# Scores and values of an attention block rebuilt: f32 keys on two row halves, probabilities stationary, row sums from a ones column

## The reference

```python
x = x + nin(attention(group_norm(x)), wo, bo)      # phase 1: softmax(q k / 8) v over all 1024 tokens
t = x.reshape(16, 1024, 64)
u = layernorm(t)
t = t + softmax(causal(u Wq (u Wk)' / 8)) u Wv      # phase 2: the same size, lower triangle only
u = layernorm(t)
logits = u gate_w' + gate_b                         # 32 experts choose 8 tokens each per image
t = t + scatter(top8 weights * ffn(top8 pooled u))
```

## Time and profile before

| | us |
|---|---|
| median of 3 runs | 1145.77 |
| lowest, highest | 1144.09, 1167.03 |
| span of the profiled execution | 1163.8 |
| PE busy | 954.6 (82%), 4402 matmuls |
| PE weight loads | 506.2 (43%) |
| DVE busy | 768.3 (66%) |
| ACT busy | 543.1 (47%) |
| POOL busy | 507.5 (44%) |

### The profile page before, as it was taken

How to read it: one execution, slowest core, us unless ns; L and a number is a source line. 1 busy time by engine, 2 the same in 40 slices (tenths; PEclk the granted TensorE clock), 3 DMA queues, 4 the chain that set the end, 5 groups by cost and what they waited for, 6 DMA issues and landing times. The chain is left out here.

```text
span 1163.8 us, 15672 instructions
## 1 busy us (share of the span) xinstructions
PE 954.6 (82%) x4402; PEld 506.2 (43%) x4402; DVE 768.3 (66%) x1741; ACT 543.1 (47%) x1110; POOL 507.5 (44%) x342
## 2 busy tenths in 40 slices
PE   2676798989798989898889989898989899876466
PEld 1333354545354544454444535454544444443235
DVE  4647677777777777776776777777766776645134
ACT  2233355565556446363545545463635455543320
POOL 0051536464646364554444454554444554642200
PEclk9987799999899879797888879797878878985657
DMA  1000000000000000010100000010100010100098
GB/s 37 0 1 9 1 10 24 10 24 10 23 9 23 9 18 14 0 32 0 32 0 23 9 20 11 0 32 0 32 0 24 9 44 16 42 1 23 24 216 238
DMA packets 58654, 30.34 MB, mean 26 GB/s; under 512 B 34775, under 2 KB 55415, under 8 KB 58623
## 3 DMA queue, kind: packets, MB, share of 16 engines
q1 hardware_dynamic: 58623, 29.95, 10.2%
HBM read 15.26 MB, written 10.49 MB: 22 GB/s over the span
## 5 line engine op out<-in xcount | busy, mean ns | idle before, releaser
L832 ACT ACTIVATE probs<-scores 128x512 f32<-128x512 f32 (+3 forms) x496 | 246.6, 513 | 302.9 <-PE scores L684 293.7
L911 POOL TENSOR_TENSOR prob_sum<-prob_sum,probs 128x1024 f32<-128x1024 f32 (+1 forms) x144 | 296.7, 2061 | 145.8 <-ACT probs L832 138.9
L1069 DVE TENSOR_REDUCE maxima<-maxima_in 128x1 f32<-128x512 f32 (+3 forms) x496 | 266.3, 580 | 78.6 <-PE maxima_in L664 75.4
L682 PE MATMUL scores<-queries_lo,keys_hi 72*128 72x512 f32 (+3 forms) x496 | 228.8, 463 | 21.9 <-DVE queries_lo L1061 21.6
L664 PE MATMUL maxima_in<-keys,queries 128*128 128x512 f32 (+3 forms) x496 | 200.3, 462 | 38.3 <-DVE maxima L1069 36.1
L684 PE MATMUL scores<-queries,keys 128*128 128x512 f32 (+3 forms) x496 | 200.0, 404 | 0.0
L698 PE MATMUL values_out<-probs,x_sb 128*64 128x512 f32 x512 | 165.1, 729 | 0.0
L664 PEld LDWEIGHTS maxima_in<-keys,queries 128*128 128x128 f32 x496 | 108.7, 227 | 125.4 <-DVE maxima L1069 71.9
L682 PEld LDWEIGHTS scores<-queries_lo,keys_hi 72*128 72x128 f32 x496 | 108.3, 218 | 105.2 <-issue 53.1
L887 POOL TENSOR_TENSOR ln<-ln,minus_half 128x8 f32<-128x8 f32 x32 | 52.7, 1648 | 187.9 <-DVE ln L1050 187.9
L684 PEld LDWEIGHTS scores<-queries,keys 128*128 128x128 f32 x496 | 108.9, 219 | 9.1
(11 more groups left out here) (167 smaller groups left out, 1244.4 us busy)
## 6 DMA issues: line engine op xcount, KB each, us to landing
x_sb<-in_x SPq DMA_DIRECT2D x16, 256.0 KB, 3.0
u_all<-u_sb SPq DMA_DIRECT2D x16, 256.0 KB, 2.4
t_scratch<-t SPq DMA_DIRECT2D x16, 256.0 KB, 2.9
total<-t_scratch SPq DMA_DIRECT2D x16, 256.0 KB, 4.6
w_sb<-in_w SPq DMA_DIRECT2D x1, 2080.0 KB
logits_scratch<-rows_mixed SPq DMA_DIRECT2D x16, 128.0 KB, 1.9
lg<-logits_scratch SPq DMA_DIRECT2D x4, 512.0 KB, 3.7
out<-total SPq DMA_DIRECT2D x16, 128.0 KB, 2.0
```

The source lines that it names most:

```text
L682: pe.matmul(bank, keys_hi[s][q][:, key_cols(t)], queries_lo[s][q][:, lo:hi], start=not diagonal, stop=False, skip_group_check=diagonal)
L832: nc.scalar.activation(probs[:, t % NP, lo:hi], scores[:, (u + (s - 1) * len(UNITS_1)) % NST, 0:hi - lo], ACT.Exp, scale=SCALE).then_inc(e ...
L911: nc.gpsimd.tensor_tensor(view(total[:, :]), view(total[:, :]), view(new), ALU.add).then_inc(rows_added, 1)
L1069: V.reduce_max(maxima[s][:, c, h:h + 1], maxima_in[:, p % NM, 0:w * P], AX.X).then_inc(maxima_taken, 1)
```

## The change

The attention is written anew; the expert part stays.

- *Scores and maxima in plain f32.* Keys lie in 64 rows twice: key tiles 0, 2, 4, 6 in the upper 64 partitions and 1, 3, 5, 7 in the lower (`keys`, 512 columns), queries in both halves. A pair of key tiles is two f32 matmuls of 64 rows, one in each half of the array, into two of three PSUM banks (L669). The row maximum comes in by a second, fp32r matmul for each (L672). No high and low parts are left, nor the instructions that made them.
- *Values.* A block of probabilities (128 keys x 128 queries) is stationary, the 64 value columns and a column of ones move (L690, 65 columns). The output has queries on partitions, and the row sums as its 65th column. `prob_sum`, POOL's sums, the copy of `values_out`, f.rs and f.out are gone; the output weights are multiplied into the values ahead (w_v, steps x.v and y.v).
- *Maxima.* Two f32 matmuls for each query tile (L652) into one buffer of two banks. DVE reduces both banks at once, in phase 2 together with an added mask (L975, L978). The maxima are turned and spread over 128 rows by PE (L628).
- *Order.* Slots are halves of a pair: 16 in phase 1 and 12 in phase 2 instead of 32 and 30. The finishing steps come in halves (f1.0, f1.1, ...), and POOL does the additions and the normalizing of layernorm in place of ACT.
- SP stores the logits of an image with two DMAs, not one.

```diff
-UNITS_1 = [(t, a, 0) for t in range(NT) for a in range(2)]
-UNITS_2 = [(t, a, j0) for t in range(NT) for a, j0 in ((0, (t + 1) // 2), (1, t // 2)) if j0 < NJ]
-UNITS = {1: UNITS_1, 2: UNITS_2}
-PIECES_1 = [(c, h, NJ) for c in range(NT) for h in range(2)]
-PIECES_2 = [(c, h, w) for c in range(NT)
-            for h, w in ((0, (2 * (c % NJ) + c // NJ) // 2 + 1), (1, (2 * (c % NJ) + c // NJ + 1) // 2)) if w]
-PIECES = {1: PIECES_1, 2: PIECES_2}
...
+PAIRS_1 = [(h, j, NJ) for h in range(2) for j in range(NJ)]
+PAIRS_2 = [(h, j, min(NJ, NJ * (h + 1) - 2 * j)) for h in range(2) for j in range(2 * (h + 1))]
+PAIRS = {1: PAIRS_1, 2: PAIRS_2}
+SLOTS = {1: 2 * len(PAIRS_1), 2: 2 * len(PAIRS_2)}
...
-    0: [("f2.rs", -2)], 2: [("p1.tr", 1)], 5: [("p1.g1", 1)], 7: [("p1.g2", 1)], 8: [("f2.out", -2)],
-    10: [("p1.w", 1), ("p1.h", 1)], 12: [("l2a", -2)], 19: [("p1.i", 1)], 22: [("l2b", -2)],
-    23: [("p1.qa", 1), ("l2c", -2)], 25: [("p1.qb", 1), ("moe.tr", -2)], 26: [("p1.ka", 1)],
-    27: [("moe.lg", -2)], 30: [("p1.kb", 1), ("r2", -1)],
+    0: [("x.tr", 1)], 1: [("f2.1", -2)], 3: [("x.g1", 1), ("l2.1", -2)], 5: [("x.g2", 1)], 6: [("r2.0", -1)],
+    7: [("x.af", 1), ("u.tr", -2)], 8: [("x.q0", 1)], 9: [("f1.0", 0), ("x.k", 1)], 10: [("x.q1", 1), ("r2.1", -1)],
+    11: [("l1.0", 0), ("x.v", 1)], 12: [("u.lg", -2)], 15: [("y.tr0", 0)],
 }
 SIDES_2 = {
-    3: [("f1.rs", 0)], 5: [("f1.out", 0), ("l1a", 0)], 7: [("l1b", 0)], 15: [("l1c", 0)],
-    19: [("p2.tr", 0)], 25: [("p2.qa", 0)], 28: [("p2.qb", 0), ("r1", 1)],
+    1: [("f1.1", 0), ("r1.0", 1)], 2: [("y.q0", 0)], 3: [("l1.1", 0), ("y.v0", 0)], 5: [("f2.0", -1)],
+    7: [("l2.0", -1), ("y.tr1", 0)], 8: [("r1.1", 1)], 9: [("y.q1", 0)], 10: [("y.v1", 0)],
 }
 SIDES = {1: SIDES_1, 2: SIDES_2}
...
+PIECE_SLOTS_1 = {2: (2, -1, 0), 3: (2, -1, 1), 4: (2, -1, 2), 5: (2, -1, 3), 6: (2, -1, 4), 7: (2, -1, 5),
+                 8: (2, -1, 6), 9: (2, -1, 7), 12: (1, 1, 0), 13: (1, 1, 1), 14: (1, 1, 2), 15: (1, 1, 3)}
+PIECE_SLOTS_2 = {1: (1, 1, 4), 3: (1, 1, 5), 5: (1, 1, 6), 7: (1, 1, 7)}
+PIECE_SLOTS = {1: PIECE_SLOTS_1, 2: PIECE_SLOTS_2}
...
-    keys = {s: [sb(f"keys{s}{q}", [P, S], F32R) for q in range(2)] for s in (1, 2)}
-    keys_hi = {s: [sb(f"keys_hi{s}{q}", [KROWS, S], F32R) for q in range(2)] for s in (1, 2)}
-    queries = {s: [sb(f"queries{s}{q}", [P, S], F32R) for q in range(2)] for s in (1, 2)}
-    queries_lo = {s: [sb(f"queries_lo{s}{q}", [KROWS, S], F32R) for q in range(2)] for s in (1, 2)}
-    probs = sb("probs", [P, NP, S])
-    prob_sum = {s: sb(f"prob_sum{s}", [P, S]) for s in (1, 2)}
-    maxima = {s: sb(f"maxima{s}", [P, NT, 2]) for s in (1, 2)}
-    neg_max = {s: sb(f"neg_max{s}", [P, NT]) for s in (1, 2)}
+    bench = ps("bench", [P, 2, HALF])
+    keys = {s: [sb(f"keys{s}{q}", [P, HALF]) for q in range(2)] for s in (1, 2)}
+    queries = {s: [sb(f"queries{s}{q}", [P, S]) for q in range(2)] for s in (1, 2)}
+    row_max = {s: sb(f"row_max{s}", [P, S], F32R) for s in (1, 2)}
+    maxima = {s: sb(f"maxima{s}", [P, NT]) for s in (1, 2)}
+    values = {s: [sb(f"values{s}{q}", [P, NT, VW]) for q in range(2)] for s in (1, 2)}
+    probs = sb("probs", [P, 2, 2, HALF])
+    masked = sb("masked", [P, 2, HALF])
+    tail_masks = sb("tail_masks", [P, 2, 2, HALF])
...
+        def piece(s, n, c):
             q = n.parity
+            w = NJ if s == 1 else c // 2 + 1
+            if s == 1 and c == 0:
+                pe.wait_ge(act_step, done("act_step", "x.q1", n, "q"))
+            if s == 2:
+                pe.wait_ge(act_step, done("act_step", f"y.q{c // NJ}", n, "q"))
+            if (s, c, n.first) == (2, 0, B - 1) and n.trip is None:
                 pe.wait_ge(g["expert_step"], done("expert_step", "e.turn", 1, "copy"))
+            v = done("maxima_taken", s, n, c) - 1
+            if n.trip is not None or v > 0:
                 pe.wait_ge(maxima_taken, v)
+            for r, part in enumerate(halves):
+                mm = pe.matmul(maxima_in[:, r, 0:w * P], queries[s][q][part, of_query(c)], keys[s][q][part, 0:w * P],
+                               start=True, stop=True)
+            mm.then_inc(maxima_ready, 1)
+        def score(s, n, p):
+            half, j, w = PAIRS[s][p]
             q = n.parity
+            cols = slice(half * HALF + (NJ - w) * P, half * HALF + HALF)
+            banks = [scores[:, (2 * p + r + s - 1) % NSB, 0:w * P] for r in range(2)]
+            if j == 0:
+                pe.wait_ge(act_step, done("act_step", f"r{s}.{half}", n, "row"))
+            diagonal = on_diagonal(s, p)
+            for r, part in enumerate(halves):
+                if exists("bank_free", s, n, 2 * p + r):
+                    pe.wait_ge(exp_done, done("bank_free", s, n, 2 * p + r))
+                if diagonal:
+                    pe.matmul(banks[r][:, r * P:(r + 1) * P], ident_b[:, :], mask_k[:, :], start=True, stop=True)
+                pe.matmul(banks[r], keys[s][q][part, j * P:(j + 1) * P], queries[s][q][part, cols],
+                          start=not diagonal, stop=False, skip_group_check=diagonal)
+            for r, part in enumerate(halves):
+                pe.matmul(banks[r], minus_64th[part, :], row_max[s][part, cols], start=False, stop=True,
+                          skip_group_check=diagonal).then_inc(scores_ready, 1)
+        def weigh(s, n, p):
+            half, j, w = PAIRS[s][p]
+            if j == 0:
+                before = out_before(s, n, half)
+                if before:
+                    pe.wait_ge(dve_step, done("dve_step", *before, "o"))
+                if s == 1 and half == 0:
+                    pe.wait_ge(dve_step, done("dve_step", "x.v", n, "v"))
+                if s == 2:
+                    pe.wait_ge(act_step, done("act_step", f"y.v{half}", n, "v"))
+            for r in range(2):
+                pe.wait_ge(exp_done, done("exp_done", s, n, 2 * p + r))
+                for k in range(r if on_diagonal(s, p) else 0, w):
+                    b = NJ - w + k
+                    mm = pe.matmul(values_out[:, b * VW:(b + 1) * VW], probs[:, p % 2, r, k * P:(k + 1) * P],
+                                   values[s][n.parity][:, 2 * j + r, :], start=j == 0 and r == 0 and k == 0,
+                                   stop=j == 2 * half + 1 if s == 2 else j == NJ - 1, skip_group_check=True)
             mm.then_inc(values_done, 1)
...
-            pe.matmul(maxima_in[:, p % NM, 0:w * P], queries[s][q][:, c * P:(c + 1) * P],
-                      keys[s][q][:, h * HALF:h * HALF + w * P], start=not diagonal, stop=True,
-                      skip_group_check=diagonal).then_inc(maxima_ready, 1)
-        def score(s, n, u):
...
-            pe.matmul(bank, keys_hi[s][q][:, key_cols(t)], queries_lo[s][q][:, lo:hi], start=not diagonal, stop=False,
-                      skip_group_check=diagonal)
-            pe.matmul(bank, keys[s][q][:, key_cols(t)], queries[s][q][:, lo:hi], start=False, stop=True,
-                      skip_group_check=diagonal).then_inc(scores_ready, 1)
...
-                mm = pe.matmul(values_out[a * C:(a + 1) * C, j0 * P:HALF], v_sb[:, t, :], probs[:, t % NP, lo:hi],
-                               start=t == 0, stop=t == NT - 1, skip_group_check=True)
...
+            elif name in ("x.q0", "x.q1"):
+                wait_to_fill(name, n, "dve_step", "x.af", n, "h")
+                mm = project(bank, w_q[1], h, half)
+            elif name == "x.k":
+                wait_to_fill(name, n, "dve_step", "x.af", n, "h")
+                mm = pe.matmul(bank[:, :], w_k[:, :], h[:, :], start=True, stop=True)
+            elif name == "x.v":
+                wait_to_fill(name, n, "dve_step", "x.af", n, "h")
+                for j in range(NJ):
+                    mm = pe.matmul(bank[:, j * P:(j + 1) * P], h[:, j * P:(j + 1) * P], w_v[1][:, :], start=True, stop=True)
...
+            elif name == "x.af":
+                dve.wait_ge(pool_step, done("pool_step", "x.g2", n, "rstd"))
+                V.tensor_tensor(affine[:, 0:1], gn[:, 7:8], const("gn_scale"), ALU.mult).then_inc(dve_step, 1)
+                after(name, n, "a")
+                V.tensor_tensor(gn[:, 8:9], gn[:, 2:3], affine[:, 0:1], ALU.mult).then_inc(dve_step, 1)
+                after(name, n, "ma")
+                V.tensor_tensor(affine[:, 1:2], const("gn_bias"), gn[:, 8:9], ALU.subtract).then_inc(dve_step, 1)
+                after(name, n, "b")
+                if exists("filled", "x.v", n + (-1)):
+                    dve.wait_ge(filled, done("filled", "x.v", n + (-1)))
+                V.tensor_scalar(h[:, :], xt[:, :], affine[:, 0:1], affine[:, 1:2], ALU.mult, ALU.add).then_inc(dve_step, 1)
...
+            if s == 1:
+                ins = V.reduce_max(maxima[1][:, c:c + 1], maxima_in[:, :, :], AX.XY)
+            else:
+                V.memset(spare[:, 1:2], 0.0)
+                ins = V.tensor_tensor_reduce(masked[:, :, 0:w], maxima_in[:, :, 0:w], tail_masks[:, c % 2, :, HALF - w:HALF],
```

(2 more changed lines are left out.)

997 lines of the change are left out of this document (457 added, 540 removed), and 16 rows, old and new, of tables (STEPS, STEPS_ACT, STEPS_DVE).

## The result

The changed kernel takes **1435.06 us** (median of four runs, 1432.05 to 1449.25). The kernel before, run beside it, has a median of 1156.4 (1144.09 to 1193.08). The ratio is 1.259, interval 1.246 to 1.272: slower by a quarter. The forecast of 1390 is 45 us short and its range of 1250 to 1520 holds the result. Over the 41 runs of it in this study, the kernel before lies between 1102.55 and 1197.87 us, with a median of 1167, and the 37 whose clock is on record differ by the granted clock (0.90 to 0.82); ratios set a kernel against runs of it at its higher clocks.

A forecast was written before the change was run, and what follows sets the result against it. Bound: PE in its written order, with its work, waits and half clock. Work 73.2, waits 3.2, clock 3.4 give a 79.8 us period, 15.0 over 64.8; 240 us over 16 images, +4 before the loop: 1390 us, range 1250 to 1520.

The forecast's parts named there:

- prologue, once: Before the loop: split chain some 10 us shorter, eight maxima pairs through one buffer some 14 longer, +4 us.
- steps 1 to 5: PE's work per image: values, maxima, scores, projections and other small products, changes of tiling; 73.2 us before any wait.
- Step 1: Values (L690): 200 passes per image, bound by weight loads at 0.1115 us each, 22.3 us against 11.1 before.
- Steps 2 and 3: Maxima (L652) 11.1 us against 5.3, scores (L668, L669, L672) 16.9 against 11.1; row halves overlap except on the diagonal.
- step 5: Changes between row halves and whole array on PE: 52 per image at 0.207 us, 10.8 us.
- The sign that was to show it: In the new profile, an open pair's two L669 start together and their successor comes 0.85 us later.
- step 6: PE waits for h in slot 8 of phase 1, some 2.4 us; with two smaller waits 3.2 us per image.
- step 7: Clock: one fall per image after a wait, 6.7 us at 1.2 GHz, half of it charged: 3.4 us.
- PE fills every gap: Rival: loads and emptying hide, no waits, clock at 2.4 GHz; period 62.5 us, 1113 us in all; chance 0.07.
- Changes cost nothing: Rival: changes of tiling are free for row halves, waits and falls stay; period 69.1 us, 1219 us; chance 0.12.
- Halves don't overlap: Rival: two 64-row matmuls do not run together in maxima and scores; period 102 us, 1748 us; chance 0.09.
- The clock does not come back: Rival: values passes stream columns half their time, a third of the time at 1.2 GHz; period 91.5, 1577 us; chance 0.10.

The follow-up runs named there:

- the kernel with the side steps first: Changed kernel with whole-array side steps ahead of the maxima pair in odd slots on PE: 1418.91 us.
- `x.af`: Changed kernel with DVE making scale, shift and h one slot earlier, slot 7 instead of 8, ahead of the reduction: 1348.69 us.
- `VW`: Changed kernel with 128 instead of 65 moving columns in the values step, the ones column repeated: 1396.41 us.
- the kernel with all edits: Changed kernel with masks first, scale/shift/h one slot earlier, side steps before maxima in odd slots, and 128 moving columns in values: 1268.7 us.
- the masks: Changed kernel with both mask matmuls of a diagonal pair ahead of its two row halves: 1362.85 us.
- its neighbour with fp32r: Changed kernel with keys and queries rounded to fp32r: 1394.56 us; the same with 128 instead of 65 moving columns in values: 1166.89 us.
- the kernel before with the later step: Kernel before with step p1.w (and p1.h) two slots later, slot 12 of phase 1 instead of 10: 1121.63 us.

## Why the prediction was right, and by which steps not

**The whole, by its terms.** The profiled spans differ by 283.7 us. 14 periods took 62.2 us each on average before and 81.0 after, which makes 263; the prologue is 6.6 longer and the last image with the expert part 13.4. The prediction had 16 x 15.0 + 4 = 244. So the period's growth was 3.8 us too small, and 14 times that is 53; luck took part of it back, since 16 periods were charged, and outside the 14 the last image with the expert part added 13.4 and not 30.

| term, us per image | predicted | measured |
|---|---|---|
| PE's work, columns, loads, changes | 73.2 | 72.7 (the 77.0 us image at clock 1.00, less 4.3 of waits) |
| waits | 3.2 | 4.5, and 1.9 more in every second image |
| falls of the clock | 3.4 | 6.0 (half of some 12 us at 1.2 GHz, partly waits) |
| period, steady | 79.8 | 83.6 (81.0 on average) |
| period before, steady | 64.8 | 64.9 (62.2 on average) |
| prologue, once | +4 | +6.6 |

**PE's work (steps 1 to 5)** is right to 1%. Step 1, the values at 0.1115 us a pass, is measured as 0.112, and the columns don't matter. The Trainium skill's rate of 81 ns for pairs of load and matmul (TensorE: Matmul & The Clock Gate, section Back-to-back issue gap) does not hold for these f32 weights; the measurement decides. Steps 2 and 3: row halves overlap. The Trainium skill says so of row groups (TensorE: Matmul & The Clock Gate, section The mechanism), and the trace now shows it. The sign that was to show it came in part: the two L669 start together, but L672 starts 0.56 us behind them and not 0.85, while their second passes run. An open pair takes 1.19 us where the sum had 1.07. The difference is the bare load of step 5 and no new term: where the same pair stands behind a maxima pair, which is tiled like it, it takes 1.09 us (112.78 to 113.87 in the kernel with the side steps first). Step 5 was mis-sized a little: 0.17 us for a change and not 0.207, with 52 of them 1.9 us too much. The 0.107 for a bare load holds on the way into row halves; before L690 it is 0.05. With this correction the terms give 71.3 us, so 1.4 us of the measured 72.7 have no term that I can name.

**Waits (step 6).** The main one came where, behind what, and as long as said: 2.4 to 2.6 us at L572 behind L933. What was missed are the waits of L690 for `t` (L952), 0.9 us at the first values of phase 1 and 0.8 at those of the second half of phase 2: the single `values_out` must be emptied by DVE before the next half may write it. I had 0.3 to 0.5 for one of the two. The wait at a turn of the loop, 1.9 us, was not foreseen at all; the kernel before has one wait of this kind, of 1.7 us, in its whole run.

**Clock (step 7)** was the step with the largest error. It charged one fall an image, 6.7 us long, as in the earlier trace rows. The kernel before has three of this length in a period from 402 us on, each at a wait (L682 at 527.8 us, L592 at 541.9, L664 at 555.9), 20.5 us in all, and its clock of 0.84 in the earlier trace rows says as much; the prediction priced the one and does not name the other two. Now the low clock lasts about 10 us behind L572, and there is a second fall at the turn of the loop:

```profile
696.96 0.88 PE L690 MATMUL values_out<-values,probs 128*128 128x65 f32 x6 [1.94 <-issue]
697.77 2.08 PE L669 MATMUL scores<-queries,keys 64*128 64x512 f32 x4
```

L669 takes 2.08 us where it takes 1.13 at full clock. The mean clock stayed between 0.80 and 1.00, the bounds that the prediction had set. The experiments on `x.af` and on `VW` show both handles: without the wait there is no fall in its place, and with 128 moving columns in L690 the clock comes back sooner or doesn't fall. What decides between the images in which it falls and those in which it doesn't stays open: the image of 77.0 us has the same wait and no fall.

**The baseline.** 64.80 us is the period from 402 us on. The six periods ahead of it took 55.3 to 64.0 us, and four of them had 4 to 9 us at the low clock in place of 20.5. I had chosen three stretches that agreed with one another and took them for the loop. It cost the forecast nothing, since the changed kernel has its shorter periods too: steady against steady the growth is 18.8 us (64.8 to 83.6), and mean against mean as well (62.2 to 81.0). Between executions it matters more: the predicted difference was laid on the median of 1145.8, and a single profiled run of this kernel says little on where its median lies.

**The rest.** The prologue was to get shorter by 10 and longer by 14; the first exponential starts at 57.0 us instead of 49.8. DVE, ACT and POOL fell to 26, 23 and 12 us (predicted 27, 25, 14), and, as said, none of this was worth anything in time, since none of them was last in line.

**The rivals.** "PE fills every gap" is out: even the kernel with all edits needs 70 us. "Changes cost nothing" is out by the 1.39 us for eight changes, at a price near that of the forecast. "Halves don't overlap" is out by the masks. "The clock does not come back" is false of this kernel and true of its neighbour with fp32r, and there the step from 65 to 128 columns bears out the reason that it gave, the sparse passes of the values.

## What to carry to other kernels

Price a matmul with a new 128-column weight by its load, not by its columns: here making the large, fresh operand stationary saved nothing, since a pass of 65 columns takes as long as one of 128. Then count the work and the clock apart, as span times granted clock and as that clock; here an edit that removed a quarter of the work returned 41 us of 310, and one that added 65 won 228. When a matmul of the whole array stands between two of separate row halves, move it out: it costs both of them their overlap.

## What the runs showed of the hardware that I had not expected

- Span times mean granted clock is the same within about 2% in all runs of a kernel, while the clock itself differs by up to 10% between runs of the same program (before: 0.82 to 0.90, 1102.55 to 1197.87 us) and by 1% in the four kernels with a clock of 0.945 and more.
- The falls of the clock looked at here begin within 2 us of a wait of PE, but a wait does not fix them: in the kernel before with the later step, 3.4 us of low clock follow a wait of 2.9 us and 17.1 us one of 1.4, and in the changed kernel a wait of 2.4 us comes with 10.2 us of low clock in one image and with none in another.
- Moving 128 instead of 65 columns, with everything else unchanged, raised the clock from about 0.92 to 0.956, and with fp32r keys and queries from about 0.72 to 0.918, for 39 and 228 us. PE's share of busy time doesn't tell this: it was 93% in the images at 0.66 and 86 to 91% in those at 1.00 and 0.88. What in those passes the clock answers to, no run here separates.
- An f32 matmul of 65 columns and one of 128 take the same time when each has new 128-column weights: 0.112 us a pass, 0.213 at the low clock.
- A change between row halves and the whole array costs 0.17 us net: 0.09 of emptying, and 0.05 to 0.10 of the next load that lies bare.
